# Attention scores in four 32-row groups of TensorE, eight steps a tile, with the normalisation on GpSimd

## The chip, the cores and the metric

The kernel runs on one core of a Trainium2 chip. The metric is the device time of one execution in microseconds (us); less is better. The core's engines are TensorE (PE in the profile; its weight loads are listed as PEld), VectorE (DVE), ScalarE (ACT), GpSimd (POOL), and SyncE (SP), which only issues transfers.

## What is computed

Two layers, each an attention part and a feed-forward part with a tanh gate, on x and a context of 64 batches of 64 channels by 256 positions. The change touches only the first attention:

```python
q = Wq @ norm(x) + bq;  k = Wk @ ctx + bk;  v = Wv @ ctx + bv      # per batch, 64 channels
# 8 heads of 8 channels; the first 4 channels of each q and k head are rotated by position
scores = q_h.T @ k_h / sqrt(8)                                      # 256 x 256 per head
out = softmax(scores) @ v_h.T
x = x + tanh(g) * (Wo @ out + bo)
```

After it come a routed expert layer, a gated attention pool and a second feed-forward part. They are not changed.

## The kernel before

**Tiles.** Two batches make one tile of 128 partitions; there are 32 tiles. A tile has 16 heads in 4 units of 4 (`u`, `j`). `column_order` puts the channels of q and k so that partition = 32 j + 4 d + u. Scores need more precision than one fp32r product gives, so q and k are split into a high and a low part and three products are added: q_hi k_hi, q_lo k_hi, q_hi k_lo.

**Stacks.** SP's transfers write the three products below each other: `q_st` has 32 rows for each product, which hold all four heads of a unit, and `k_st` has the same 96 rows once for each head, zero where the row is another head's. So one matmul over 96 rows gives the scores of one head (L510, into `s_ps`). VectorE takes the maximum of each row (L369). The maxima, negated and split, are turned by TensorE (L461), copied by ScalarE (L409) and written as 8 more rows of `q_st`. The second pass, transposed (L527, into `st_ps`, 104 rows), has the maximum subtracted and goes to ScalarE's exponential (L422, into `e_t`). The values are multiplied with it in L546: 32 output rows per head, four heads in the four column groups of the array. A column of ones in `v_st` gives the sums of the softmax. `o_ps` is copied (L414), turned (L488), divided (L352, L356), turned back (L494), copied (L399), projected (L441), scaled (L403) and added to x by GpSimd (L254). The projections of q and k are L433, of v L471; their rotation is L295, their split on GpSimd L260, L268, L270.

**Order.** `body(n, c, i)` on every engine is a fixed list of 16 steps `s_`; bodies run for n = -2 to 33, and are a loop unrolled four times in between. Body n computes maxima for tile n+1 (one pair of heads in every other step, L510), transposed scores for tile n (one head a step, `LAG` = 8 steps into the body), projections for tile n+2, and the output of tile n-1. All projections, turns and the output use one PSUM bank, `misc`, in turn. `s_ps` and `st_ps` have two buffers each, `e_t` eight. Every engine executes its list in order, so a wait holds up all that is behind it. SP's list of a body: the context of tile n+3, the maxima rows of tile n, then 6 of the k transfers, 3 of q and 6 of k for tile n+2. GpSimd's list: variance and rstd of tile n+2, the addition to x of tile n-2, the split of k, the split of q.

Of the kernel before, what the change touches and what calls it, by code (L numbers as in the profile page):

```python
# [67 lines left out]
def attention(nc, dram, x, ident, tanh_gain):  # L68
# [6 lines left out]

    HP = 2 * HEADS
    LAG = 8
    ROWS, MROWS = 96, 104
    PEEL_FIRST, PEEL_LAST = (-2, -1, 0, 1), (30, 31, 32, 33)

    with ExitStack() as ctx:
# [6 lines left out]
        def sem(name):  # L88
# [4 lines left out]
        bias = sb("bias", [P, 5])  # L93
        bias_v = sb("bias_v", [P, P])
        rope = sb("rope", [P, 2, D])
        own_head = sb("own_head", [P, UH])
        gains = sb("gains", [P, 4])
        out_bias = sb("out_bias", [P, 1])
        half = sb("half", [P, 1])

# [4 lines left out]
        rstd = sb("rstd", [P, 1])  # L105
        xn = sb("xn", [P, D])
        roped = {a: sb(f"{a}_roped", [P, 2, D]) for a in "qk"}
        whole = {a: sb(f"{a}_whole", [P, D]) for a in "qk"}
# [7 lines left out]
        e_t = [sb(f"e_t{r}", [P, 2, D]) for r in range(8)]  # L116
# [6 lines left out]
        s_ps = [ps(f"s_ps{r}", [P, 4, D]) for r in range(2)]  # L123
        st_ps = [ps(f"st_ps{r}", [P, 2, D]) for r in range(2)]
# [4 lines left out]
        x_first_in, x_rest_in = sem("x_first_in"), sem("x_rest_in")  # L129
        c_loaded = [sem(f"c_loaded{r}") for r in range(RING)]  # L130
        q_stacked = [sem(f"q_stacked{r}") for r in range(RING)]
        k_stacked = [[sem(f"k_stacked{j}_{r}") for r in range(RING)] for j in range(UH // 2)]
        m_stacked = [sem(f"m_stacked{r}") for r in range(RING)]
        names = ("values_cleared first_cleared others_cleared ones_set own_set tanh_ready bias_ready half_set "
                 "stats_raw stats_done eps_added rstd_ready xn_ready "
                 "q_projected q_roped q_summed q_high q_split k_projected k_roped k_summed k_high k_split "
# [27 lines left out]
        def st_head(s_):  # L164

            return (0, s_ - LAG) if s_ >= LAG else (-1, s_ + LAG)

# [3 lines left out]
        def _(sp):  # L171
# [3 lines left out]
            for dst, src in ((w_in[:], dram["w_in"]), (bias[:], dram["bias"]), (rope[:], dram["rope"]),  # L175
                             (own_head[:], dram["own_head"])):
                sp.dma_start(dst, src).then_inc(consts_in, 16)
            sp.dma_start(x[:, 0:4, :], rows[:, 0:4, :]).then_inc(x_first_in, 16)
            for dst, src in ((bias_v[:], dram["bias_v"]), (gains[:], dram["gains"]), (ident[:], dram["ident"]),
                             (w_out[:], dram["w_out"])):  # L180
                sp.dma_start(dst, src).then_inc(more_consts_in, 16)

            def body(n, c, i):
# [6 lines left out]
                if isinstance(n, int) and n == -2:  # L190
                    for t in range(4, TILES, 14):
                        sp.dma_start(x[:, t:t + 14, :], rows[:, t:t + 14, :]).then_inc(x_rest_in, 16)
                if there(n, c, 0):
                    r = c % RING
                    sp.wait_ge(s["m_taken"], n + 1)

                    sp.dma_start(q_st[r][ROWS:MROWS, :, :].bitcast(F32),
                                 m_rows[:, :].bitcast(F32)).then_inc(m_stacked[r], 16)
                if there(n, c, 2):
                    r = (c + 2) % RING  # L200

                    wait_count(sp, s["st_scored"], HP * (n - 1))
                    wait_alone(sp)

                    if isinstance(n, int) and n == -2:
                        sp.wait_ge(s["first_cleared"], 2)
                    if isinstance(n, int) and n == 0:
                        sp.wait_ge(s["others_cleared"], 2)

                    def stack_k(j, t, of):  # L210
                        sp.dma_start(k_st[r][32 * t + 8 * j:32 * t + 8 * j + 8, :, j, :].bitcast(F32),
                                     part["k"][32 * j:32 * j + 32, of, :].bitcast(F32)).then_inc(k_stacked[j // 2][r], 16)

                    sp.wait_ge(s["k_high"], n + 3)
                    for j in range(2):
                        stack_k(j, 0, 0)
                        stack_k(j, 1, 0)
                    sp.wait_ge(s["k_split"], n + 3)  # L220
                    for j in range(2):
                        stack_k(j, 2, 1)
                    sp.wait_ge(s["q_split"], n + 3)
                    for t, of in enumerate((0, 1, 0)):
                        sp.dma_start(q_st[r][32 * t:32 * t + 32, :, :].bitcast(F32),
                                     part["q"][:, of, :].bitcast(F32)).then_inc(q_stacked[r], 16)
                    for j in range(2, UH):
                        for t, of in enumerate((0, 0, 1)):
                            stack_k(j, t, of)
# [4 lines left out]
        def _(pool):  # L234
            nc.gpsimd.memset(half[:], -0.5).then_inc(s["half_set"], 1)
            nc.gpsimd.memset(y_sb[:], 0.0).then_inc(s["y_free"], 1)
            for r in (0, 1):
                nc.gpsimd.memset(k_st[r][0:ROWS, :, :, :].bitcast(F32), 0.0).then_inc(s["first_cleared"], 1)
            pool.wait_ge(s["half_set"], 1)

            def body(n, c, i):
                if there(n, c, 2):
                    pool.wait_ge(s["stats_done"], n + 3)

                    wait_count(pool, s["xn_ready"], n + 2)
# [9 lines left out]
                for a in "kq":  # L255
                    if there(n, c, 2):
# [6 lines left out]
                        if there(n, c, 1):  # L263

                            for of_ring in stacked:
                                pool.wait_ge(of_ring[before], (48 if a == "q" else 96) * uses(c, i, 1))
# [1910 lines left out]
```

## Time and profile before

| | us |
|---|---|
| median of 3 runs | 1567.44 (1565.45 to 1570.59) |
| the profiled execution, its own time | 1564.62 |
| its span, first to last instruction | 1562.6 |
| the first attention in it | 0 to 586 |
| mean granted TensorE clock | 0.958 of full speed |

Busy over the span: PE 93%, PEld 77%, DVE 61%, ACT 50%, POOL 34%. A busy share of PE counts matmuls whose ends are modelled, and overlapping ones once.

### The profile page before, as it was taken

The numbers are of one execution on the slowest core, as the hardware profiler recorded it, in microseconds if no ns is written. First come the engines' busy times: TensorE is split into PE (matmuls) and PEld (weight loads), VectorE is DVE, ScalarE is ACT, GpSimd is POOL, SyncE is SP. The second block draws the span as 40 slices with busy tenths as digits, with TensorE's granted clock in tenths as the row PEclk, the third lists the DMA queues.
The fourth block names the chain that finished last, engine by engine and source line by source line (L and its number), as shares of the span: only waits on it lengthen the run. The fifth ranks groups of instructions, "written<-read, shape, count | busy, mean of one in ns | idle before, by whom it ended". The sixth has DMA issues, their size and how long they took to land. (4 is left out here: it accounts for less than half of the span.)

```text
span 1562.6 us, 32056 instructions
## 1 busy us (share of the span) xinstructions
PE 1451.1 (93%) x10096; PEld 1209.4 (77%) x10097; DVE 953.7 (61%) x1817; ACT 775.4 (50%) x1425; POOL 535.0 (34%) x592
## 2 busy tenths in 40 slices
PE   3999999999999986999988999999978699999998
PEld 2777777777777755888877888888867478888887
DVE  7888887888788734776655433333324466666653
ACT  4466666666666663333223333333332656666652
POOL 4332332332333201744455443320005344455220
PEclk9999999999999995999999999999995799999999
DMA  5122122112212202211265332221125001111000
GB/s 176 57 57 62 53 55 62 54 53 62 55 52 62 54 3 77 105 41 55 71 196 190 121 94 91 91 67 54 50 57 175 27 28 41 42 42 41 15 14 28
DMA packets 89081, 106.54 MB, mean 68 GB/s; under 512 B 12208, under 2 KB 80432, under 8 KB 88368
## 3 DMA queue, kind: packets, MB, share of 16 engines
q1 hardware_dynamic: 79264, 73.60, 15.9%
q0 software_dynamic: 9744, 31.99, 6.4%
q8 instruction: 43, 0.70, 0.2%
q14 instruction: 30, 0.25, 0.0%
HBM read 54.29 MB, written 25.03 MB: 51 GB/s over the span
## 5 line engine op out<-in xcount | busy, mean ns | idle before, releaser
L422 ACT ACTIVATE e_t<-st_ps 128x512 f32<-128x512 f32 x512 | 277.9, 595 | 165.7 <-PE st_ps L527 165.2
L369 DVE TENSOR_REDUCE row_max<-s_ps 128x4 f32<-128x1024 f32 x256 | 311.0, 1217 | 32.5 <-PE s_ps L510 32.4
L510 PE MATMUL s_ps<-k_st,q_st 96*128 96x256 f32 x1024 | 196.7, 315 | 13.0 <-DMA q_st<-q_part 11.7
L527 PE MATMUL st_ps<-q_st,k_st 104*128 104x256 f32 x1024 | 170.2, 287 | 1.6 <-ACT e_t L422 1.5
L510 PEld LDWEIGHTS s_ps<-k_st,q_st 96*128 96x128 f32 x1024 | 147.4, 193 | 21.9 <-DMA q_st<-q_part 12.5
L527 PEld LDWEIGHTS st_ps<-q_st,k_st 104*128 104x128 f32 x1024 | 143.6, 189 | 6.6 <-ACT e_t L422 5.2
L546 PE MATMUL o_ps<-e_t,v_st 128*32 128x256 f32 x2048 | 137.0, 385 | 0.9 <-ACT e_t L422 0.9
L1599 POOL DMA_INDIRECT gathered_tail<-sorted_results,result_at x64 | 70.1, 1095 | 153.7 <-POOLq L2090 135.4
L1457 PE MATMUL y_ps_moe<-w_all_moe,xt_hi_moe 128*128 x568 | 113.3, 283 | 3.8 <-DVE xt_lo_moe L1276 3.8
L1836 DVE TENSOR_TENSOR h_all_tail<-silu_tail,u_ps_tail 128x512 f32<-128x512 f32 x64 | 43.9, 685 | 115.5 <-ACT silu_tail L1707 65.1
L1282 DVE TENSOR_TENSOR h_all_moe<-silu_moe,u_ps_moe 128x512 f32<-128x512 f32 x71 | 48.8, 687 | 107.2 <-PE u_ps_moe L1435 107.2
L1435 PE MATMUL g_ps_moe<-w_all_moe,xt_hi_moe 128*128 x284 | 107.0, 418 | 0.0
L972 ACT COPY y_sb_moe<-y_ps_moe 128x256 f32<-128x256 f32 x71 | 26.4, 372 | 161.4 <-PE y_ps_moe L1457 161.4
L1435 PE MATMUL u_ps_moe<-w_all_moe,xt_hi_moe 128*128 x284 | 99.8, 392 | 0.0
L1457 PEld LDWEIGHTS y_ps_moe<-w_all_moe,xt_hi_moe 128*128 128x128 f32 x568 | 92.8, 190 | 7.4 <-issue 4.7
L1272 DVE TENSOR_TENSOR xt_lo_moe<-t_ps_moe,xt_hi_moe 128x256 fp32r<-128x256 f32 x71 | 30.1, 424 | 93.2 <-ACT xt_hi_moe L959 93.0
L820 POOL DMA_INDIRECT sorted_rows<-xn_moe,slots_moe x64 | 64.6, 1009 | 62.7 <-DVE slots_moe L1075 45.5
L247 POOL TENSOR_SCALAR var_eps<-mean_var 128x1 f32<-128x1 f32 x32 | 7.5, 233 | 229.4 <-DVE mean_var L310 228.3
L546 PEld LDWEIGHTS o_ps<-e_t,v_st 128*32 128x32 f32 x2048 | 53.5, 109 | 40.1 <-ACT e_t L422 1.1
L1457 PE MATMUL y_ps_moe<-w_all_moe,xt_lo_moe 128*128 x284 | 80.1, 282 | 0.0
L1707 ACT ACTIVATE silu_tail<-g_ps_tail 128x512 f32<-128x512 f32 x64 | 38.0, 594 | 82.4 <-PE g_ps_tail L1995 82.3
L2007 PE MATMUL y_ps_tail<-w_hi_tail,h_hi_tail 128*128 128x256 f32 x256 | 73.5, 287 | 0.5 <-DVE h_lo_tail L1843 0.5
(310 smaller groups left out, 3592.6 us busy)
## 6 DMA issues: line engine op xcount, KB each, us to landing
k_st<-k_part SPq DMA_DIRECT2D x384, 32.0 KB
q_st<-q_part SPq DMA_DIRECT2D x96, 128.0 KB, 3.2
stage_moe<-in_experts POOLq DMA_DIRECT2D x21, 512.0 KB, 4.3
rows_in_moe<-sorted_rows SPq DMA_DIRECT2D x71, 128.0 KB, 2.0
sorted_results<-y_sb_moe SPq DMA_DIRECT2D x71, 128.0 KB
c_in<-in_ctx SPq DMA_DIRECT2D x33, 128.0 KB, 2.1
xn_moe<-in_ctx SPq DMA_DIRECT2D x8, 512.0 KB
context_tail<-in_ctx SPq DMA_DIRECT2D x8, 512.0 KB, 10.9
```

Source lines behind the costliest of these rows:

```text
L369: nc.vector.tensor_reduce(out, s_ps[s_ // 2 % 2][:].rearrange("p (j h) t -> p j h t", j=2), AX_X, ALU.max).then_inc(s["max_taken"], 1)
L422: nc.scalar.activation(e_t[h % 8][:], st_ps[h % 2][:], ACT.Exp, scale=float(DH) ** -0.5)\
L510: last = nc.tensor.matmul(s_ps[s_ // 2 % 2][:, 2 * (h - s_) + half_, :], q_st[r][0:ROWS, u, half_ * P:(half_ + 1) * P], k_st[r][0:ROWS, u, ...
L527: last = nc.tensor.matmul(st_ps[h % 2][:, half_, :], k_st[r][0:MROWS, u, j, half_ * P:(half_ + 1) * P], q_st[r][0:MROWS, u, :], start=True ...
L546: last = nc.tensor.matmul(o_ps[32 * j:32 * j + 32, u % 2, :], v_st[r][:, half_, u * UH + j, :], e_t[(u * UH + j) % 8][:, half_, :], start= ...
L820: pool.indirect_dma_start(out=xs[:, :], out_offset=bass.IndirectOffsetOnAxis(ap=slots[:, w, GT * j + t:GT * j + t + 1], axis=0), in_=xn[j ...
L1282: nc.vector.tensor_tensor(h_all[c % 2][:], silu[c % 2][:], u_ps[c % 2][:], ALU.mult)\
L1435: last = nc.tensor.matmul(bank[c % 2][:], t[b][:, kc * P:(kc + 1) * P], w_flat[:, bass.ds(where + ((w * 3 + kc) * PIECE + base), FF)], sta ...
L1457: last = nc.tensor.matmul(y_ps[:, 2 * ((c - 1) % 2), :], h[:, m * P:(m + 1) * P], w_flat[:, bass.ds(where + ((w * 3 + 2) * PIECE + m * D), ...
L1599: pool.indirect_dma_start(out=gathered[r][:], out_offset=None, in_=ys[:, :], in_offset=bass.IndirectOffsetOnAxis(ap=result_at[:, q // GT, ...
L1836: nc.vector.tensor_tensor(h_all[m % 2][:], silu[m % 2][:], u_ps[n % 2][:], ALU.mult)\
L2007: last = nc.tensor.matmul(y_ps[:, t, :], h[:, m, t * P:(t + 1) * P], w[:, m * D:(m + 1) * D], start=(m == 0 and b == 0 and t % 2 == 0), st ...
```

## The change

In words: the stacks are laid out by head. Rows 32 j to 32 j + 31 of `q_st` and `k_st` belong to head j of a unit: 8 channels by four rows, which are q_hi k_hi, q_lo k_hi, q_hi k_lo, and for two of the 8 channels a fourth row with the maxima (a zero in `q_st` until they are known, a one in `k_st`). A score is then a matmul over 32 rows, and heads j lie in different row groups of the array. A body has 8 steps. In each, TensorE issues eight score matmuls: for each half of the positions two transposed ones (heads of tile n, `LAG` = 5) and two plain ones (heads of tile n+1), whose four row groups and four PSUM banks differ. Then come 4 value matmuls (half a unit; 8 instructions, as each fp32 one is two), then one of the other jobs. `st_ps` has now one buffer, of two heads, and the exponential covers 128 x 1024. `k_st` shrinks from 4096 to 1024 columns, `k` takes 3 transfers a tile, not 12, `q` 3 and a small one of zeros.

Off VectorE: the normalised x (two GpSimd operations, one tile earlier), the bias of q and k (added on GpSimd, `turned_bias`), the two additions of the v bias (v is copied by ScalarE; its bias goes through `w_out` into `out_bias`). The two rotations of q, and of k, are one operation of 512 columns each. GpSimd's list is now: split of k, split of q, addition to x, normalisation of tile n+3.

```diff
-    LAG = 8
+    STEPS = HP // 2
+    LAG = 5
+    MAX_ROWS = slice(3, P, 16)
...
-        k_st = [sb(f"k_st{r}", [P, UNITS, UH, D], F32R) for r in range(RING)]
+        k_st = [sb(f"k_st{r}", [P, UNITS, D], F32R) for r in range(RING)]
...
-        st_ps = [ps(f"st_ps{r}", [P, 2, D]) for r in range(2)]
+        st_ps = ps("st_ps", [P, 2, 2, D])
...
@@ SP, body
+                if there(n, c, 2):
+                    wait_count(sp, s["st_scored"], STEPS * (n - 1))
+                    sp.dma_start(q_st[r][MAX_ROWS, :, :].bitcast(F32), zero_rows[:, :, :].bitcast(F32))
...
                     sp.wait_ge(s["k_high"], n + 3)
+                    for t in range(2):
+                        sp.dma_start(k_st[r][t:P:4, :, :].bitcast(F32), part["k"][:, 0, :].bitcast(F32))
...
+                    sp.wait_ge(s["q_high"], n + 3)
+                    for t in (0, 2):
+                        sp.dma_start(q_st[r][t:P:4, :, :].bitcast(F32), part["q"][:, 0, :].bitcast(F32))
...
@@ GpSimd
+            def normalize(n, k):
+                pool.wait_ge(s["stats_done"], n + k + 1)
+                nc.gpsimd.tensor_tensor(like_row(n, centered), x_row(n + k), mean_var[:, 0:1] ..., ALU.subtract)
+                nc.gpsimd.tensor_scalar(var_eps[:], mean_var[:, 1:2], EPS, None, ALU.add)
+                nc.gpsimd.tensor_tensor(rstd[:], var_eps[:], half[:], ALU.pow)
+                wait_count(pool, s["q_projected"], n + k)
+                nc.gpsimd.tensor_tensor(xn[:], centered[:], rstd[:].to_broadcast([P, D]), ALU.mult)
...
             def body(n, c, i):
+                    parts_of("k", n, c, i)
+                    parts_of("q", n, c, i)
...
+                    pool.wait_ge(s["y_taken"], n - 1)
+                    nc.gpsimd.tensor_tensor(row, row, like_row(n, y_sb), ALU.add)
...
+                    normalize(n, 3)
@@ VectorE
+                nc.vector.tensor_tensor(roped[a][:].rearrange("p a t -> p (a t)"), misc[:],
+                                        rope[:].rearrange("p a t -> p (a t)"), ALU.mult)
...
+                for p in range(STEPS):
+                    if p == 0 and there(n, c, 0): split_max(n, c)
+                    if there(n, c, 1): take_max(n, c, p)
+                    if p == 0 and there(n, c, 2): rope_parts("k", n, c)
+                    if p == 2 and there(n, c, 2): rope_parts("q", n, c)
+                    if p == 4 and there(n, c, -1): normalize_out(n, 0)
+                    if p == 5 and there(n, c, 3): stats_of(n, 3)
+                    if p == 7 and there(n, c, -1): normalize_out(n, 1)
@@ ScalarE: the exponential comes first in each step; then
+                    p == 1: m_rows; p in (2, 6): o_sb; p == 3: a_t; p == 5: y_sb; p == 6: v_st (copy 128x256)
@@ TensorE
+            def score_step(n, c, i, p):
+                if turned:
+                    wait_count(pe, s["exp_done"], STEPS * (n + k) + t)
+                    wait_alone(pe)
+                if plain:
+                    if p == 0:
+                        pe.wait_ge(q_stacked[(c + 1) % RING], 64 * uses(c, i, 1))
+                        pe.wait_ge(k_stacked[(c + 1) % RING], 48 * uses(c, i, 1))
+                    wait_count(pe, s["max_taken"], (n + 1) * STEPS + p - 1)
+                for at in range(0, 4, 2):
+                    for of, done in ((turned, "st_scored"), (plain, "scored")):
+                        for out, w, moving in of[at:at + 2]:
+                            last = nc.tensor.matmul(out, w, moving, start=True, stop=True)
...
+                for p in range(STEPS):
+                    score_step(n, c, i, p)
+                    use_values(n, c, p)
+                    p == 0: k projection; 1: turn the maxima; 2: q projection; 3: turn a_sb;
+                    p == 4: turn o_sb[0]; 5: output projection; 6: v projection; 7: turn o_sb[1]
```

The lines of the diff that name several steps `p` in one line are shortened from separate `if` blocks. The first bodies also differ: VectorE clears all `k_st` (1024 columns each) and makes the rotated biases; GpSimd clears `q_st`.

## Rows read from the trace of the kernel before

**Rows 1.** Stretches of the span, as one table

```profile
core 0: us, PE busy (x) PEld busy (x) DVE busy (x) ACT busy (x) POOL busy (x), PEclk, DMA share, GB/s
0.00:24.00 24.00, 5.35 (x12) 3.30 (x13) 14.63 (x21) 15.69 (x6) 11.89 (x16) 1.00 0.83 249
200.00:500.00 300.00, 297.58 (x2730) 234.75 (x2722) 243.18 (x409) 191.87 (x376) 92.32 (x160) 1.00 0.21 56
556.00:586.00 30.00, 24.18 (x219) 14.67 (x217) 5.41 (x15) 19.84 (x40) 2.14 (x3) 0.99 0.01 2
575.00:586.00 11.00, 6.36 (x55) 3.34 (x53) 1.10 (x4) 4.91 (x10) 0.67 (x1) 0.97 0.00 1
586.00:1562.00 976.00, 901.29 (x5200) 780.98 (x5200) 503.55 (x1070) 415.94 (x747) 360.59 (x297) 0.94 0.23 73
```

**Rows 2.** One line, 200 to 500 us: duration, first and last start

```profile
L409 ACT CAST m_rows<-misc x18: 252/254/255, 211.3 to 498.6; 64x128 fp32r<-64x128 f32 x18
```

**Rows 3.** Groups by line and shape, 200 to 500 us

```profile
L369 DVE TENSOR_REDUCE row_max<-s_ps 128x4 f32<-128x1024 f32 x143 | 174.0, 1217 | 16.3 <-PE s_ps L510 16.3
L422 ACT ACTIVATE e_t<-st_ps 128x512 f32<-128x512 f32 x286 | 155.2, 595 | 92.8 <-PE st_ps L527 92.8
L546 PE MATMUL o_ps<-e_t,v_st 128*32 128x256 f32 x1152 | 77.1, 385 | 0.0
L414 ACT COPY o_sb<-o_ps 128x512 f32<-128x512 f32 x36 | 21.1, 585 | 6.0 <-PE o_ps L546 4.3
L399 ACT COPY a_t<-misc 128x256 f32<-128x256 f32 x18 | 6.7, 372 | 10.0 <-PE misc L494 10.0
L403 ACT ACTIVATE y_sb<-misc,out_bias,tanh_gain 128x256 f32<-128x256 f32 x18 | 10.2, 569 | 0.0
L295 DVE SCALAR_TENSOR_TENSOR k_roped<-misc,bias,rope 128x256 f32<-128x256 f32 x36 | 15.8, 480 | 9.0 <-PE misc L433 9.0
```

**Rows 4.** Timeline, TensorE matmuls: start us, length us, what

```profile
301.08 1.07 PE L546 MATMUL o_ps<-e_t,v_st 128*32 128x256 f32 x16
302.50 0.72 PE L510 MATMUL s_ps<-k_st,q_st 96*128 96x256 f32 x4
303.05 0.64 PE L527 MATMUL st_ps<-q_st,k_st 104*128 104x256 f32 x4
...
309.84 1.13 PE L433 MATMUL misc<-c_in,w_in 128*128 128x256 f32 x4
310.62 0.82 PE L510 MATMUL s_ps<-k_st,q_st 96*128 96x256 f32 x4
```

**Rows 5.** Timeline, TensorE weight loads beside them

```profile
301.08 0.59 PEld L546 LDWEIGHTS o_ps<-e_t,v_st 128*32 128x32 f32 x16
302.08 0.42 PEld L488 LDWEIGHTS misc<-ident,o_sb 128*128 128x128 f32 x4 [0.41 <-issue]
```

**Rows 6.** Timelines of ScalarE, PEld and PE, end of the stage

```profile
561.98 1.09 ACT L422 ACTIVATE e_t<-st_ps 128x512 f32<-128x512 f32 x2
...
562.63 0.30 PEld L527 LDWEIGHTS st_ps<-q_st,k_st 104*128 104x128 f32 x2 [0.69 <-ACT e_t L422]
...
577.71 0.74 PE L527 MATMUL st_ps<-q_st,k_st 104*128 104x256 f32 x4
...
578.25 1.09 ACT L422 ACTIVATE e_t<-st_ps 128x512 f32<-128x512 f32 x2 [0.84 <-PE st_ps L527]
```

**Rows 7.** The groups again, GpSimd, 200 to 500 us

```profile
L260 POOL TENSOR_TENSOR k_whole<-k_roped 128x256 f32<-128x256 f32 x18 | 13.2, 732 | 23.2 <-DVE k_roped L295 23.2
L249 POOL TENSOR_TENSOR rstd<-var_eps,half 128x1 f32<-128x1 f32 x18 | 10.2, 568 | 1.5
```

**Rows 8.** DMA issues, 200 to 500 us, with median us to landing

```profile
q_st<-q_part SPq DMA_DIRECT2D x54, 128.0 KB, 3.2
```

**Rows 9.** Waits, 200 to 500 us: total us, times, longest

```profile
ACT e_t L422 <- PE st_ps L527: 92.8, 125, 1.9
```

**Rows 10.** The page, its costliest groups

```profile
L1836 DVE TENSOR_TENSOR h_all_tail<-silu_tail,u_ps_tail 128x512 f32<-128x512 f32 x64 | 43.9, 685 | 115.5 <-ACT silu_tail L1707 65.1
```

More of the change, by code:

```diff
@@ L205, in body @@
[L205 to L212, printed above, removed]
@@ L223, in body @@
-                    sp.wait_ge(s["q_split"], n + 3)
[L224 to L229, printed above, removed]
+                    sp.dma_start(k_st[r][2:P:4, :, :].bitcast(F32), part["k"][:, 1, :].bitcast(F32))\
+                        .then_inc(k_stacked[r], 16)
@@ L248, in body @@
[L248 to L249 removed]
+                    parts_of("k", n, c, i)
+                if there(n, c, 2):
+                    parts_of("q", n, c, i)
                 if there(n, c, -2):
                     pool.wait_ge(s["y_taken"], n - 1)
[L252 to L253 removed]
@@ L273, in _ @@
+                    row = x_row(n - 2)
+                    nc.gpsimd.tensor_tensor(row, row, like_row(n, y_sb), ALU.add).then_inc(s["y_free"], 1)
+                if there(n, c, 3):
+                    normalize(n, 3)
             steps(pool, body)
@@ L435, in project, with scores @@
                 last.then_inc(s[a + "_projected"], 1)
-            def body(n, c, i):
-                for s_ in range(HP):
-                    if s_ == 0 and there(n, c, -2):
-                        pe.wait_ge(s["a_taken"], n - 1)
-                        nc.tensor.matmul(misc[:, 0:D], w_out[:], a_t[:], start=True, stop=True)\
-                            .then_inc(s["y_projected"], 1)
-                    if s_ == 2 and there(n, c, 2):
-                        if isinstance(n, int) and n < 2:
+            def scores(c, p):
+                r = (c + 1) % RING
+                for half_ in range(2):
+                    for at in range(2):
+                        u, j = (2 * p + at) // UH, (2 * p + at) % UH
+                        rows = slice(32 * j, 32 * j + 32)
+                        yield (s_ps[p % 2][:, at, half_, :], q_st[r][rows, u, half_ * P:(half_ + 1) * P],
+                               k_st[r][rows, u, :])
@@ new lines, in body @@
+                    if p == 4 and there(n, c, -1):
+                        if there(n, c, -2):
+                            pe.wait_ge(s["a_taken"], n - 1)
+                        else:
+                            pe.wait_ge(s["q_roped"], n + 3)
+                        pe.wait_ge(s["o_taken"], 2 * (n - 1) + 1)
+                        turn_out(0)
+                    if p == 5 and there(n, c, -2):
+                        pe.wait_ge(s["a_taken"], n - 1)
+                        if there(n, c, -1):
+                            pe.wait_ge(s["o_normed"], 2 * (n - 1) + 1)
+                        nc.tensor.matmul(misc[:, 0:D], w_out[:], a_t[:], start=True, stop=True)\
+                            .then_inc(s["y_projected"], 1)
@@ L552, in _, with value_bias @@
-            steps(pe, body)
+                        pe.wait_ge(s["o_normed"], 2 * (n - 1) + 1)
+                        pe.wait_ge(s["o_taken"], 2 * n)
+                        turn_out(1)
+            def value_bias():
+                pe.wait_ge(more_consts_in, 3 * 16)
+                pe.wait_ge(s["v_stored"], 1)
+                nc.tensor.matmul(misc[:, 0:1], w_out[:], bias[:, 5:6], start=True, stop=True)\
+                    .then_inc(s["value_bias_made"], 1)
+            steps(pe, body, None, value_bias)
```

500 lines of the change are left out of this document (248 added, 252 removed).

## The prediction, made before the changed kernel was run

> **What bounds the kernel now.** I read the stretches first, then the groups of the steady stretch, then its timeline, then the end of the stage. The stretches [rows 1] show that the first attention ends at 586 us and that the 976 us after it have nothing to do with the change. From 200 to 500 us TensorE is busy 297.6 of 300 us, VectorE 243.2, ScalarE 191.9, GpSimd 92.3, at full clock. One tile takes (498.6 - 211.3) / 17 = 16.90 us [rows 2]. ScalarE waits 92.8 us of these 300, all for the transposed scores [rows 9]; TensorE waits for nobody. So TensorE's own list is the bound, and I have to take it apart.
>
> Busy time does not do that, since matmuls overlap; distances between starts do. Four score matmuls take 303.05 - 302.50 = 0.55 us, 0.14 each [rows 4]; 64 a tile are 8.8 us. A burst of 16 value matmuls takes 1.00 us, from its start at 301.08 to the next load at 302.08 [rows 4, 5]; four a tile are 4.0. What is left, 4.1 us, is the eight other jobs with the changes between them: a projection of k or q takes 310.62 - 309.84 = 0.78 each [rows 4], which leaves (4.1 - 1.56) / 6 = 0.42 for each of the other six.
>
> **What the rows say of tiling the array.** A value matmul lasts 385 ns [rows 3], yet 16 of them fit in 1.07 us [rows 4]: four column groups really work side by side. At the end of such a burst the loads stand still for 0.41 us before the next job can load [rows 5]. That is the price of leaving the column groups, and the change makes twice as many such bursts. Row groups do not occur in this trace. Their gain has to be bounded: from none (0.14 us a matmul) to the four at a time of the column groups. I take four at a time, since the nearest row is the same array used in 32-wide groups, and the change sends each round to four different banks. [...]
>
> **The change, part by part: TensorE.** Eight scores go out in two rounds of four. After a wait, two score matmuls one after the other lead to the start of the exponential in 578.25 - 577.71 = 0.54 us [rows 6]; two rounds should take the same, and some hundredths for the stagger, 0.56. The next job's loads can begin about 0.1 before, at 0.45. A value burst is now half as long and there are eight. Its price lies between half of 1.00 = 0.50 and half of the loads plus the whole stand, 0.30 + 0.41 = 0.71 [rows 5]; I take 0.60. The other job costs 0.78 at steps 0 and 2 and 0.42 at the rest. Going back to row groups costs something between 0 and 0.41; I take 0.25. Sums: 0.45 + 0.60 + 0.25 + 0.78 = 2.08 us at steps 0 and 2, 1.72 at the other six: 14.5 us a tile.
>
> **ScalarE's loop.** `st_ps` has one buffer now. So exponential, next scores, next exponential form a chain. The exponential of 1024 columns: a copy of 256 takes 372 ns, of 512 585 [rows 3], so 213 for 256 more; 595 + 2 x 213 = 1.02 us. After an exponential TensorE loads 0.05 later: the first of the two that begin at 561.98 ends at 562.575, the load starts at 562.63 [rows 6]. So 1.02 + 0.05 + 0.56 = 1.63 us a step at least, 13.0 a tile. This lies below TensorE's 1.72, so TensorE's list decides, but only just. ScalarE's other work has 0.05 + 0.56 = 0.61 us in each step, while the scores are made. `o_sb` (0.585) fits, `y_sb` (0.569) nearly; at step 6 `o_sb` and the new copy of v come to 0.585 + 0.37 = 0.96 (v as the copy of 256 columns to `a_t`, [rows 3]), so the next exponential starts 1.02 + 0.56 + 0.96 = 2.54 us after the scores began, which means a step of 1.98, 0.26 more than 1.72. Together 14.5 + 0.26 = 14.8 us a tile. The extra wait on VectorE's maximum that now stands ahead of the transposed matmuls too is held at nothing, as `s_ps` has two buffers and VectorE is a step behind at most.
>
> **VectorE.** It loses the normalised x and the v additions. What stays: eight maxima at 1.217 = 9.7 us [rows 3], two rotations of 512 PSUM columns at 0.685 [rows 10], where four of 0.48 stood [rows 3]. The rest (statistics, split, division) I take from the difference: 243.2 us in 300 are 13.7 a tile; 13.7 - 9.7 - 4 x 0.48 = 2.1, from which the removed ones come off. So VectorE needs 11.1 to 13.2 us. That is cover, not bound, if TensorE comes at 14.8; it is the next in line.
>
> **GpSimd.** Nine operations on 256 columns at 0.73, two copies at no more, rstd 0.57 [rows 7]: 8 to 9.2 us a tile. It has the time. Its order matters: k and q are split ahead of the addition, which waits for step 5. q is rotated about 2.8 us after the start of step 2; add, add, copy, subtract at up to 0.73 end 2.9 later; the stack lands 3.2 after [rows 8]. That is 8.9 us, plus an issue or two, about 10 after step 2 starts; the next body starts 14.8 - 2.08 - 1.72 = 11.0 after it. One us of slack. Had the addition come first, it would have held q to the end of step 5, 3 or 4 us later. The transfers carry what they carried, in 9 issues and not 17, so SP's queue gets shorter.
>
> **Start and end.** To 24 us only twelve matmuls run [rows 1]; large clears of `k_st` and twelve small k transfers stand ahead. They shrink, the new clears and bias operations add some back. I take 6 us off, between 0 and 12. At the end (556 to 586, [rows 1]) the chain of one buffer replaces two; I take no change.
>
> **The sum.** (16.90 - 14.8) x 30 full tiles = 63; with 6 at the start, 69 us. The profiled execution took 1564.62 (span 1562.6 and 2.0 around it) and would be 1496. The median is 2.8 above it, 1567.4 - 69 = 1498.
>
> **Rival 1: the switches cost more.** The trace's 0.41 of standing loads [rows 5] speaks for it. [...] Price: 0.27 us at each of the two changes that I held at nothing or at 0.25, so a step is 0.45 + 0.27 + 0.60 + 0.27 + other job, 12.7 + 4.1 = 16.8 us a tile with all, or 16.1 where the other jobs' 4.1 already holds their part. At 16.1: 1567 - 24 - 6 = 1537. At 0.41 each it would pass 16.9 and end slower. [...]
>
> **Rival 2, slower: row groups load one after the other.** What decides is whether a load of 128 weight columns can run beside another row group's. Value loads have only 32 columns, so the rows do not prove it. If they cannot, eight scores go at 0.14: the sixth ends 0.54 + 4 x 0.14 = 1.10 after the start, and ScalarE's loop is 1.02 + 0.05 + 1.10 = 2.17. TensorE: 0.45 + 6 x 0.14 = 1.29, with 0.60 + 0.25 makes 2.14 + other job, 17.1 + 4.1 = 21.2 us a tile at worst, 19.5 if the changes cost nothing. At 19.5: 1567 + 78 - 6 = 1639. It turns slower as soon as the scores take (16.9 - 14.8) / 8 = 0.26 us a step longer than two rounds.
>
> **Rival 3: better.** If a half value burst costs 0.50 and the return to row groups nothing, ScalarE's chain decides: 13.0 plus 0.35 at step 6 and 0.5 at steps 0 and 2; 13.6 a tile gives 1567 - 99 - 6 = 1462. The q chain of 10 us after step 2 would then have no slack left, so it cannot be much less.
>
> **Rival 4: q comes late, or nothing changes.** If GpSimd runs slower beside VectorE, body starts wait for `q_stacked` and the tile stays near 16.9: 1561.
>
> **The clock.** TensorE will have gaps of tenths of a us in each step. It had such at the end of the stage, 58% busy, at a granted clock of 0.97 [rows 1]. [...]
>
> **How the numbers follow.** Forecast 0.60 (tile 14.2 to 15.5), rival 1 0.16, rival 2 0.11, rival 3 0.10, rival 4 0.03. Range: from rival 3's 1462 to 1550, which takes in most of rival 1. Left out: rival 2, rival 4, the ends. A measurement here can tell 0.3% (4.7 us) from no change. Faster: 0.60 + 0.10 + 0.15 = 0.85; same: 0.03; slower: 0.12.
>
> **What would show it.** Right: score matmuls starting in fours a few ns apart, 16 value loads become 8, the restart of scores 0.05 after an exponential, copies of `m_rows` 14.8 us apart, exponential near 1.02 us, VectorE's maxima never waited for long. Wrong: score matmuls 0.1 or more apart (rival 2), idle loads of 0.3 us at most changes (rival 1), TensorE waiting for q's transfers at body starts (rival 4), or a clock under 0.9 in the stage.

## The result, and the profile after

The changed kernel took 1518.99 us (median of 4 runs, 1517.46 to 1523.47) beside 1567.76 for the kernel before: ratio 0.969, 95% interval 0.967 to 0.972. It is 48.8 us faster where 69 were forecast. The profiled execution took 1523.47, with a span of 1521.6.

The stretches of the changed kernel answer to [rows 1]; its first attention ends at 539 us, not 586 (columns as there).

```profile
24.00:54.00 30.00, 24.34 (x129) 14.89 (x127) 24.41 (x29) 5.10 (x7) 14.26 (x24) 0.62 0.20 66
200.00:500.00 300.00, 271.89 (x3068) 140.66 (x3068) 251.69 (x358) 208.85 (x282) 149.99 (x249) 1.00 0.20 63
...
500.00:506.00 6.00, 4.33 (x51) 2.16 (x47) 2.85 (x6) 4.30 (x6) 0.46 (x1) 0.98 0.01 3
506.00:533.00 27.00, 26.01 (x159) 11.31 (x160) 1.65 (x6) 14.34 (x17) 0.73 (x1) 0.50 0.01 2
533.00:540.00 7.00, 2.99 (x18) 1.32 (x18) 0.55 (x2) 2.09 (x4) 1.45 (x2) 0.99 0.00 0
```

TensorE now has gaps (271.9 of 300 us, before 297.6) and the other engines are busier. The granted clock is lower in two stretches. While the stage starts it is 0.62 on average, where the kernel before had 0.89 in the same window:

```profile
24.00:54.00 30.00, 22.49 (x121) 17.87 (x121) 24.93 (x37) 4.14 (x9) 9.01 (x16) 0.89 0.23 61
```

From 506 to 533 us, where only the last exponentials and their values are left, it is 0.50. The clock records of every trace here hold 1.00 or 0.50 and nothing else, so a mean such as 0.62 is a mixture of the two.

The copies of `m_rows` answer to [rows 2]:

```profile
L423 ACT CAST m_rows<-misc x17: 246/246/247, 207.5 to 449.0; 64x128 fp32r<-64x128 f32 x17
```

A tile takes (449.0 - 207.5) / 16 = 15.09 us, before 16.90. The last of these 16 are no longer bodies of the loop: bodies 26 to 33 are written out behind it, and they are shorter. From copy to copy the loop alone takes (389.4 - 207.5) / 12 = 15.16, the written-out bodies (477.9 - 434.5) / 3 = 14.47. This difference is used below. The groups by line and shape, 200 to 500 us (answering to [rows 3]):

```profile
L361 DVE TENSOR_REDUCE row_max<-s_ps 128x4 f32<-128x1024 f32 x162 | 197.8, 1221 | 31.2 <-PE s_ps L498 30.1
L417 ACT ACTIVATE e_t<-st_ps 128x1024 f32<-128x1024 f32 x161 | 165.0, 1025 | 88.7 <-PE st_ps L498 86.6
L514 PE MATMUL o_ps<-e_t,v_st 128*32 128x256 f32 x1288 | 102.9, 391 | 0.0
L498 PE MATMUL st_ps<-q_st,k_st 32*128 32x256 f32 x644 | 80.6, 325 | 28.1 <-ACT e_t L417 17.5 <-DVE row_max L361 7.4
L342 DVE TENSOR_TENSOR q_roped<-misc,rope 128x512 f32<-128x512 f32 x19 | 13.1, 691 | 7.0 <-PE misc L456 7.0
L266 POOL TENSOR_TENSOR xn<-centered,rstd 128x256 f32<-128x256 f32 x19 | 11.7, 616 | 1.5
```

One step in the timeline (answering to [rows 4, 5]; start, length, what, and the idle time ahead of it with its releaser):

```profile
300.67 0.18 PEld L498 LDWEIGHTS st_ps<-q_st,k_st 32*128 32x128 f32 x2 [0.33 <-DVE row_max L361]
300.67 0.38 PE L498 MATMUL st_ps<-q_st,k_st 32*128 32x256 f32 x2
300.67 0.18 PEld L498 LDWEIGHTS s_ps<-k_st,q_st 32*128 32x128 f32 x2
300.67 0.39 PE L498 MATMUL s_ps<-k_st,q_st 32*128 32x256 f32 x2
300.77 0.19 PEld L498 LDWEIGHTS st_ps<-q_st,k_st 32*128 32x128 f32 x2
...
300.89 0.28 PE L498 MATMUL st_ps<-q_st,k_st 32*128 32x256 f32 x2
300.90 0.28 PE L498 MATMUL s_ps<-k_st,q_st 32*128 32x256 f32 x2
...
301.11 0.64 PE L514 MATMUL o_ps<-e_t,v_st 128*32 128x256 f32 x8
301.21 1.02 ACT L417 ACTIVATE e_t<-st_ps 128x1024 f32<-128x1024 f32 x1 [0.58 <-PE st_ps L498]
...
301.68 0.20 PEld L561 LDWEIGHTS misc<-ident,a_sb 128*128 128x128 f32 x2 [0.41 <-DVE q_roped L342]
...
302.46 0.19 PEld L498 LDWEIGHTS st_ps<-q_st,k_st 32*128 32x128 f32 x2 [0.59 <-issue]
```

Four score matmuls start together, the next four 0.22 us later, and the burst of values after 0.44 us. The exponential begins at 301.21 and ends at 302.24, but the next scores load at 302.46, about 0.23 later. That gap matters below.

**Where the time went** (spans, before to after). The first copy of `m_rows` comes at 39.8 and not at 43.1 us: -3.3. From the first to the last copy 465.8 and not 519.8 us: -54.0 (forecast -63). From the last copy to the end of the stage 33.7 and not 23.1: +10.6. All that follows: 982.2 and not 976.6: +5.6. Together -41.0. The medians lie 48.8 apart, since the profiled execution of before was among the fastest of its kernel and that of after was the slowest of its four.

### The profile page after: what moved, and what is told of

Its sections match the earlier page's. It is cut to its first block and busy times, and to the rows that moved or that the text cites. A ratio compares the mean times of both kernels' runs of the same rounds, so it can differ in the third digit from the quotient of the medians.

```text
span 1521.6 us, 31047 instructions
## 1 busy us (share of the span) xinstructions
PE 1372.3 (90%) x10098; PEld 1025.4 (67%) x10099; DVE 919.2 (60%) x1665; ACT 751.9 (49%) x1197; POOL 616.3 (41%) x722
## 5 line engine op out<-in xcount | busy, mean ns | idle before, releaser
L417 ACT ACTIVATE e_t<-st_ps 128x1024 f32<-128x1024 f32 x256 | 262.3, 1025 | 154.1 <-PE st_ps L498 151.0
L498 PE MATMUL st_ps<-q_st,k_st 32*128 32x256 f32 x1024 | 132.9, 336 | 48.9 <-ACT e_t L417 30.9
L514 PE MATMUL o_ps<-e_t,v_st 128*32 128x256 f32 x2048 | 169.8, 404 | 0.0
L498 PEld LDWEIGHTS st_ps<-q_st,k_st 32*128 32x128 f32 x1024 | 81.1, 190 | 121.5 <-issue 72.5
L498 PE MATMUL s_ps<-k_st,q_st 32*128 32x256 f32 x1024 | 131.4, 338 | 8.5 <-DMA q_st<-q_part 6.5
L1333 DVE TENSOR_TENSOR h_all_moe<-silu_moe,u_ps_moe 128x512 f32<-128x512 f32 x71 | 48.8, 687 | 108.6 <-PE u_ps_moe L1486 108.3
L498 PEld LDWEIGHTS s_ps<-k_st,q_st 32*128 32x128 f32 x1024 | 78.0, 190 | 12.3 <-DMA q_st<-q_part 6.8
L995 ACT ACTIVATE silu_moe<-g_ps_moe 128x512 f32<-128x512 f32 x32 | 19.1, 598 | 107.1 <-PE g_ps_moe L1404 107.1
L1018 ACT ACTIVATE silu_moe<-g_ps_moe 128x512 f32<-128x512 f32 x71 | 42.5, 599 | 59.6 <-PE g_ps_moe L1486 59.5
```

Of the source, the lines that this page charges most:

```text
L417: nc.scalar.activation(e_t[t % 4][:], st_ps[:], ACT.Exp, scale=float(DH) ** -0.5)\
L498: last = nc.tensor.matmul(out, w, moving, start=True, stop=True)
L514: last = nc.tensor.matmul(o_ps[32 * j:32 * j + 32, u % 2, :], v_st[r][:, half_, u * UH + j, :], e_t[(2 * u + j // 2) % 4][:, j % 2, half_, :],
L1333: nc.vector.tensor_tensor(h_all[c % 2][:], silu[c % 2][:], u_ps[c % 2][:], ALU.mult)\
```

## The experiments

The edits are made to the changed kernel. The medians stand with the ratio to the kernel before; the tile is the distance between copies of `m_rows` from 200 to 450 us. An edit that adds or takes away lines shifts the line numbers.

**Same row group back to back.**

```diff
-                for at in range(0, 4, 2):
-                    for of, done in ((turned, "st_scored"), (plain, "scored")):
-                        for out, w, moving in of[at:at + 2]:
+                for of, done in ((turned, "st_scored"), (plain, "scored")):
+                    if of:
+                        for out, w, moving in (of[0], of[2], of[1], of[3]):
```

> The eight score matmuls of a step are issued with the two of one row group behind each other, so five slots are needed instead of two. Theory A (the gain comes from four row groups at once): each step's scores take 0.33 us longer on TensorE and the transposed ones end 0.11 later; the steps' copies of the maxima go from 15.15 us apart to about 17.7, the time from 1519 to about 1600. Rival (row groups add little, the gain is that of eight longer steps and less VectorE work): no more than 0.3 us a tile, under 1530.

1527.3 us, 0.974 [0.971, 0.978]; a tile of 15.2. The number is the rival's (under 1530), but it does not speak against the row groups, since the edit did not take the concurrency away. The timeline tells why:

```profile
299.88 0.39 PE L498 MATMUL st_ps<-q_st,k_st 32*128 32x256 f32 x2 [0.50 <-ACT e_t L417]
299.90 0.39 PE L498 MATMUL s_ps<-k_st,q_st 32*128 32x256 f32 x2
300.10 0.28 PE L498 MATMUL st_ps<-q_st,k_st 32*128 32x256 f32 x2
300.12 0.28 PE L498 MATMUL s_ps<-k_st,q_st 32*128 32x256 f32 x2
```

The program issues all four transposed matmuls ahead of the plain ones. In the trace the plain ones of the free row groups start 0.02 us after the first two, ahead of the transposed ones issued before them. Matmuls of different row groups overtook each other here, so the order of issue inside a step was no handle on the concurrency. The row groups themselves have to be changed. (The median is 8 us above the changed kernel's; between the first and last copy of `m_rows` the traces differ by 1.9 us, and the rest was not traced.)

**Two row groups, and one.** These two compute scores of the wrong heads: heads 2 and 3 get those of heads 0 and 1, and with one group all four get head 0's. The work is the same.

```diff
-rows = slice(32 * j, 32 * j + 32)
+rows = slice(32 * (j % 2), 32 * (j % 2) + 32)
```

With one group it is `j % 1`.

> Heads 0 and 2 use row group 0, heads 1 and 3 row group 1 (scores of the wrong heads for half of them): four rounds of two. Theory A: a step's scores 0.24 us longer on TensorE, 0.12 to 0.24 later for the exponential; a tile about 16.7 us, the time about 1569, as before the change. Rival: 15.1 us, 1519.

> All score matmuls read rows 0 to 31, so all eight of a step are in one row group and heads 1 to 3 of a unit get head 0's scores; everything else is as in the change. Theory A (four at a time is the gain): eight turns of 0.12 us, TensorE's step 0.71 us longer, the exponential starts 1.0 us after the first load instead of 0.54; a tile about 20.5 us, the time about 1686, slower than before. Rival (the row groups are not what counts): 15.1 us, 1519.

Two groups: 1557.31 us (ten runs, 1553 to 1578), 0.995 [0.992, 0.999], tile 16.3. One group: 2037.37, 1.297 [1.293, 1.300], tile (416.9 - 225.0) / 6 = 32.0. Timeline of two groups, then of one, then the stretch from 200 us of one:

```profile
300.71 0.38 PE L498 MATMUL st_ps<-q_st,k_st 32*128 32x256 f32 x2
300.93 0.28 PE L498 MATMUL s_ps<-k_st,q_st 32*128 32x256 f32 x2
301.05 0.28 PE L498 MATMUL st_ps<-q_st,k_st 32*128 32x256 f32 x2
301.16 0.29 PE L498 MATMUL s_ps<-k_st,q_st 32*128 32x256 f32 x2
301.38 0.64 PE L514 MATMUL o_ps<-e_t,v_st 128*32 128x256 f32 x8
```

```profile
300.03 0.79 PE L498 MATMUL st_ps<-q_st,k_st 32*128 32x256 f32 x2
300.62 0.62 PE L498 MATMUL s_ps<-k_st,q_st 32*128 32x256 f32 x2
301.05 0.62 PE L498 MATMUL st_ps<-q_st,k_st 32*128 32x256 f32 x2
301.47 0.62 PE L498 MATMUL s_ps<-k_st,q_st 32*128 32x256 f32 x2
302.03 1.08 PE L514 MATMUL o_ps<-e_t,v_st 128*32 128x256 f32 x8
```

```profile
200.00:500.00 300.00, 299.39 (x1423) 191.64 (x1423) 121.39 (x168) 101.33 (x130) 70.99 (x119) 0.53 0.10 31
```

With two groups a step needs four rounds of two, and first load to value burst is 0.67 us and not 0.44. The tile is 1.25 us longer for it, and of the 1.81 us gained a tile 0.56 are left. So most of the gain of the change is the step from two row groups to four, as forecast. With one group the matmuls go one by one, 0.21 apart, but this is not the price of the missing groups alone: the granted clock is 0.53, so most of the stretch ran at the lower level, 0.50 (the value burst shows it too, 1.08 us for 0.64). The expectation had the full clock and missed by 350 us. Early in the same trace, from 62.7 to 66.1 us, the granted clock was 1.00 (a value burst takes 0.64 us there), and one step shows the price of the groups by itself:

```profile
64.70 0.47 PE L498 MATMUL st_ps<-q_st,k_st 32*128 32x256 f32 x2 [0.17 <-ACT e_t L417]
...
65.81 0.82 PE L514 MATMUL o_ps<-e_t,v_st 128*32 128x256 f32 x8
```

Eight scores take 1.11 us and not 0.44, that is 2.5 times as long; the 0.67 more are near the 0.71 that the expectation had for it. So in this step, at full clock, the price of the groups was as expected. The tile of 32.0 us was taken at a clock of 0.53; how its excess over the expected 20.5 divides between the clock and the rest was not measured.

**The order of the waits.** The changed kernel waits for the exponential, then for VectorE's maximum. In the loop the counts of both waits are computed from the loop's index, in the written-out bodies they are constants. Between the two waits stands a `nop`. The author's estimate was that the restart of the scores, 0.23 us after the exponential, pays for a count computed behind the first wait; no view of the profile lists such work, so only the times can speak for it. Turned round:

```diff
                 if turned:
-                    wait_count(pe, s["exp_done"], STEPS * (n + k) + t)
-                    wait_alone(pe)
                 if plain:
...
                     wait_count(pe, s["max_taken"], (n + 1) * STEPS + p - 1)
+                    wait_alone(pe)
+                if turned:
+                    wait_count(pe, s["exp_done"], STEPS * (n + k) + t)
```

> TensorE waits for VectorE's maximum first, alone, and for the exponential in front of the first score matmul itself. Theory A (ScalarE's chain of 1.025 + 0.225 + 0.54 us a step decides, and 0.17 of the 0.225 is TensorE's sequencer working out the second count after the wait): restart after an exponential falls to 0.05 to 0.11 us, a tile in the loop from 15.15 to 14.3 +- 0.2, the time by about 20 us to 1499. Theory B (VectorE, busy 252 of 300 us, decides): no change, within 3 us of 1519.

The 0.17 us in it is an estimate: about the 0.225 of the changed kernel's trace less the 0.05 of [rows 6]. What the traces show in its place follows below, 0.12 and 0.06.

1486.75 us, 0.948 [0.945, 0.951]: 32 us better than the changed kernel, and more than expected. The tile is (436.1 - 210.8) / 16 = 14.08. Its timeline:

```profile
301.46 1.02 ACT L417 ACTIVATE e_t<-st_ps 128x1024 f32<-128x1024 f32 x1 [0.67 <-PE st_ps L498]
...
302.54 0.18 PEld L498 LDWEIGHTS st_ps<-q_st,k_st 32*128 32x128 f32 x2 [0.39 <-ACT e_t L417]
```

The exponential ends at 302.48 and the scores load 0.06 later. The medians lie 32 us apart, the two profiled spans 38.7: of these 28.6 lie between the first and the last copy of `m_rows`, 5.3 between the last and the end of the stage, where the low clock lasted for 7 us and not 27, and 4.7 behind the stage. Step by step, worked out from the single instructions of the traces (median over 16 tiles, us: length of the step, and from the end of the exponential to its first load):

```
step                     0     1     2     3     4     5     6     7    sum
changed, length       2.07  1.80  2.07  1.80  1.76  1.88  1.80  1.91  15.08
changed, after exp    0.34  0.50  0.23  0.50  0.23  0.19  0.23  0.23
turned round, length  2.07  1.62  2.07  1.62  1.68  1.72  1.65  1.65  14.08
turned round, after   0.05  0.50  0.05  0.50  0.05  0.11  0.05  0.08
```

The steps 0 and 2, which hold a projection and where TensorE's list decides, are the same. The six others were bound by ScalarE's loop, which had become 1.02 + 0.54 + 0.23 = 1.79 us; they fall to 1.62 to 1.72. The length of step 7 contains the gap of 0.34 ahead of step 0, where the waits for the stacks also stand behind the first one.

The edit moved the `nop` as well as the count, so by itself it does not tell which of them cost the time. The written-out bodies of the changed kernel do: they have the same waits in the same order with the same `nop`, but every count is a constant.

```profile
471.42 1.02 ACT L417 ACTIVATE e_t<-st_ps 128x1024 f32<-128x1024 f32 x1
...
472.56 0.21 PEld L498 LDWEIGHTS st_ps<-q_st,k_st 32*128 32x128 f32 x2
```

There the scores load 0.11 us after the exponential (the most frequent gap of the three tiles from 436 to 478 us), in the loop 0.23, with the waits turned round 0.05. So 0.12 of the 0.18 us is the difference between bodies of the loop and bodies with constant counts (0.23 and 0.11), and 0.06 that between the two orders (0.11 and 0.05), with the `nop` and the second wait behind the exponential or ahead of it. Ahead of step 0 it is 0.34 in the loop and 0.22 behind it, again 0.12.

**The waits apart.** The transposed matmuls wait for the exponential only and go first; then the wait on the maximum and the plain ones.

```diff
                 if turned:
                     wait_count(pe, s["exp_done"], STEPS * (n + k) + t)
+                    for out, w, moving in turned:
+                        last = nc.tensor.matmul(out, w, moving, start=True, stop=True)
                 if plain:
                     wait_count(pe, s["max_taken"], (n + 1) * STEPS + p - 1)
+                    for out, w, moving in plain:
+                        last = nc.tensor.matmul(out, w, moving, start=True, stop=True)
```

> In each step the four transposed score matmuls go first and wait for the exponential alone; then the four plain ones wait for VectorE's maximum. No wait stands ahead of another any more. If the order of the two waits is all that e2 changed (the count worked out after the exponential), e12 comes out as e2: tile 14.08 us, 1487. If VectorE's maxima also held up the transposed scores in e2, e12 is below it, 13.8 or less, 1478. If the plain matmuls now come too late to share the rounds, above it: 14.4 or more, 1497.

1493.98 us, 0.954 [0.952, 0.956], tile 14.4, 7 us worse than turning them round and the third of the three cases of the expectation. The second wait with its count now stands between the two groups, and the plain matmuls start 0.09 us after the transposed ones (301.51 after 301.42 in one step) and not 0.01, the value burst begins 0.52 and not 0.44 us after the first load, and the steps 0 and 2, bound by TensorE, take 2.26 and 2.16.

**Fewer switches.** With the waits turned round, values in bursts of 16 in every other step.

```diff
+                    if t % 2 == 0:
+                        return
                     pe.wait_ge(s["exp_done"], STEPS * (n + k) + 2 * u + 2)
-                    for j in range(UH):
+                    for half_ in range(2):
+                        for j in range(UH):
...
```

> The wait order of e2, and the value matmuls of a whole unit in one burst of 16 every other step, so four entries into the column groups and four stands fewer a tile. If the changes of the array's shape are what TensorE (busy 241 of 250 us in e2) loses: two half bursts of 0.57 become one of 1.00, 0.57 us a tile less on its list, the tile from 14.08 to about 13.6, the time about 1473. Rival (ScalarE's chain and VectorE decide; a burst of 1.00 in one step makes that step late): 14.1 us or more, 1487 or more.

1537.06 us, 0.978 [0.975, 0.982], tile 15.7: worse than eight bursts by 1.6 us a tile. The steps with a burst take 2.50 (0 and 2), 2.02 and 2.08, the ones without fall to ScalarE's 1.62 and no lower, with one of 1.70. So four switches fewer gained nothing here. The long bursts fell in the even steps, on top of the two projections; in the odd steps they were not tried. An estimate from the same rows for that, 4 x 2.05 + 4 x 1.62 = 14.7 us, still lies above the 14.08 of eight bursts.

**The end of the stage.** For n = 31 and 32, where no maxima are left to take, four idle score matmuls are added to each step; nobody reads them.

```diff
+                if isinstance(n, int) and n in (31, 32):
+                    if (n, p) == (31, 0):
+                        pe.wait_ge(s["max_taken"], TILES * STEPS)
+                        wait_alone(pe)
+                    for out, w, moving in scores(c, p):
+                        nc.tensor.matmul(out, w, moving, start=True, stop=True)
```

> In bodies 31 and 32, where no plain scores are left, each step issues four score matmuls more into the idle s_ps, whose result nobody reads. Theory C (the stage's last 33.7 us, from the last copy of the maxima to its end, are 10 us longer than before because the granted clock fell to 0.5 there when the plain scores stopped): clock 1.0 down to the last steps, the end 24 us, the time 1509. Rival (the single st_ps buffer makes the end long): clock may stay but the end keeps 30 us or more, the time 1517 to 1521.

1513.5 us, 0.965 [0.962, 0.968]; from the last copy of `m_rows` to the end 27.0 us and not 33.7. Its stretch:

```profile
506.00:533.00 27.00, 19.97 (x232) 9.90 (x232) 2.20 (x8) 16.29 (x23) 2.07 (x3) 1.00 0.01 2
```

More matmuls (232 for 159), less busy time, full clock: work that nobody needs makes the kernel faster. So at least 6.7 of the 10.6 us went with the low clock. Why 27.0 and not 23.1 is open; one buffer for `st_ps` is a candidate, and it wasn't tried.

**Both.** Waits turned round and the busy end.

> The wait order of e2 and the extra matmuls of e4 together. If the two gains are of different places they add: tile 14.08 us, the end of the stage from 28.4 to about 24, the time about 1482 (e2: 1486.75; e4 took 5.5 off). Rival: e2's end had most of its clock already, so nothing is added, 1487.

1484.18 us, 0.945 [0.943, 0.947], the lowest median, though the 2.6 us to the turned waits alone lie inside the spread of the runs. The busy end is worth little here (26.4 us for 28.4), since with the waits turned round the clock fell for 7 us only, 492.8 to 499.6.

**VectorE as cover.** One more `bn_stats` of 0.42 us a tile, its result unused, on the changed kernel and on the one with the waits turned round.

```diff
+                nc.vector.bn_stats(spare[:], x_row(n + k)).then_inc(s["spare_made"], 1)
```

> The change with one more statistics operation a tile on VectorE (0.42 us and its wait), result unused. Theory A (VectorE is cover, idle 2.4 us of a 15.15 us tile): under 0.1 us a tile, under 1522. Theory B (VectorE decides): 0.42 us a tile or more, 1532 or more.

> The same extra VectorE operation in e2, where VectorE is busy 223.9 of 250 us, idle 1.5 us of a 14.08 us tile. Theory A: under 0.15 us a tile, under 1491.5. Theory B: once the wait order is mended VectorE decides, 0.42 us a tile, about 1500.

1515.56 us, 0.967 [0.965, 0.970], tile 15.09; and 1492.2, 0.951 [0.948, 0.953], tile 14.08. Neither tile moved, so VectorE, busy for 251.7 of 300 us in the changed kernel, is cover in both. Whether the change had needed to take the normalisation and the v additions off VectorE was not tested; this shows only that 0.42 us more would fit. The second is 5 us above its base, and its end shows where:

```profile
478.00:505.00 27.00, 26.43 (x160) 11.14 (x156) 1.65 (x6) 14.36 (x18) 0.73 (x1) 0.50 0.01 2
```

The end ran at the low clock again, 34.0 us for 28.4. Small shifts decide whether it does.

**GpSimd's order.** The addition to x ahead of the split of q, as it stood in the kernel before (there it was ahead of the split of k too). The normalisation stays on GpSimd.

```diff
-                if there(n, c, 2):
-                    parts_of("q", n, c, i)
                 if there(n, c, -2):
...
                     nc.gpsimd.tensor_tensor(row, row, like_row(n, y_sb), ALU.add).then_inc(s["y_free"], 1)
+                if there(n, c, 2):
+                    parts_of("q", n, c, i)
```

> GpSimd adds to x ahead of the split of q, as the old order had it. Theory A (the q chain then starts at step 5's end: y_sb ends 11.9 us after a body's start, add 0.73, four operations 3.1, transfers about 3.2): TensorE waits at each body start for q's transfers, a tile takes about 18.9 us, the time about 1635. Rival (transfers are hidden anyway): 15.15 us, 1519.

1668.56 us, 1.063 [1.059, 1.067], tile (439.0 - 213.4) / 11 = 20.5. Waits, 200 to 500 us: total, times, longest:

```profile
PE st_ps L498 <- DMA q_st<-q_part: 52.2, 15, 3.6
```

Once a tile TensorE waits 3.5 us for q's transfer; the prediction had q held up by 3 or 4. And TensorE is busy for 236.0 us of 300 at a mean clock of 0.83, which the expectation (1635) did not have: the low clock is part of the 20.5. The order is worth 150 us, what the clock cost included: without it the change would lose.

## Why the prediction was right, and by how much it was off

**Direction and mechanism: right.** The row groups do work four at a time, in the changed kernel's timeline, and two experiments that took them away lost most or all of the gain. A score went from 0.14 us [rows 4] to 0.44 / 8 = 0.055, 2.5 times the rate; with one row group at full clock it was 1.11 / 8 = 0.14 again. Rival 2 (loads one after the other) is out: the first four loads all start at 300.67 in the timeline above, the next four 0.10 later. Whether the four different banks of a round have a part in it was not tested.

**TensorE's terms: right to 0.03 us.** Scores 0.44 (0.45 forecast), half a value burst 0.57 (0.60), a k projection with the return to row groups 311.98 - 310.92 = 1.06 (0.78 + 0.25 = 1.03), step 0 2.07 (2.08). Exponential 1.025 (1.02), first load to exponential 0.54 (0.56).

**The restart after the exponential: wrong, the costliest term in the loop.** It was taken as 0.05, from [rows 6]: the kernel before, at the end of its stage, where the transposed matmuls wait for the exponential and no second wait comes behind it. In the changed kernel's loop it was 0.23, and 0.34 ahead of step 0. The same error stands a second time in the prediction, where the extra wait on VectorE's maximum was "held at nothing": not because a maximum came late, but because a second wait stands behind the exponential's, with a count computed in the loop. What was measured: turning the waits round took 1.0 us off the tile, all of it in the six light steps and none in the two that TensorE bounds, and the written-out bodies, with constant counts, restart after 0.11 with the order unchanged and take 14.47 us a tile for 15.16. The profile names VectorE's `row_max` as the releaser of these loads, or "issue"; a wait for several semaphores is put down to the last event. The step table speaks against the maximum: with its wait ahead of the exponential's the restart fell from 0.23 to 0.05.

**Step 6 and the light steps: too dear.** With the gap gone the six light steps take 9.94 us together; forecast 6 x 1.72 + 0.26 = 10.58. The 0.26 at step 6 did not appear: in ScalarE's timeline of the changed kernel

```profile
306.64 1.02 ACT L417 ACTIVATE e_t<-st_ps 128x1024 f32<-128x1024 f32 x1
...
307.57 0.58 ACT L428 COPY o_sb<-o_ps 128x512 f32<-128x512 f32 x1
...
308.03 0.39 ACT L444 COPY v_st<-misc 128x256 f32<-128x256 f32 x1
...
308.44 1.03 ACT L417 ACTIVATE e_t<-st_ps 128x1024 f32<-128x1024 f32 x1
```

`o_sb` begins 0.09 us before the exponential ends and `v_st` 0.12 before `o_sb` ends, so both fit while the scores of 307.90 are made. The sum added whole lengths. The forecast of 1.72 for TensorE's list was also some hundredths above the 1.62 to 1.72 measured. The two errors partly cancelled, and that the tile came so near, 15.09 against 14.8, is in part luck: 54.0 us from the first to the last copy, where the sum had 63.

**The end: held at nothing, was +10.6 us.** The prediction allowed for no fall of the clock, from a stretch with TensorE 58% busy at 0.97. In the changed kernel it was granted 0.50 over 27 us in that part of the stage; with idle matmuls added it was 1.00 and the end 6.7 us shorter. At the start, where -3.3 came of the -6, the clock was low too, until 55.2 us by the clock's records, before until 42.6. What that cost was not separated. The traces whose clock records reach back that far have it too, until 55 to 67 us, and in the others the column's 1.00 is no evidence against it. The run with one more statistics operation on the changed kernel, its stretch and two projections of k and q:

```profile
24.00:54.00 30.00, 25.00 (x127) 15.31 (x125) 25.01 (x31) 5.10 (x7) 14.26 (x24) 1.00 0.20 66
...
36.25 2.08 PE L460 MATMUL misc<-c_in,w_in 128*128 128x256 f32 x4
...
56.93 1.13 PE L460 MATMUL misc<-xn,w_in 128*128 128x256 f32 x4
```

Four matmuls of one shape take 2.08 and later 1.13 us. The changed kernel's trace, whose clock records reach back that far, shows both lengths beside both levels, 2.08 inside the stretch at 0.50 (to 55.2 us) and 1.13 behind it:

```profile
31.30:55.20 23.90, 19.96 (x113) 12.12 (x117) 19.10 (x24) 5.10 (x7) 10.71 (x19) 0.50 0.24 76
55.20:62.00 6.80, 5.79 (x69) 2.94 (x73) 5.51 (x6) 4.72 (x6) 4.92 (x8) 1.00 0.19 63
...
52.38 2.08 PE L456 MATMUL misc<-c_in,w_in 128*128 128x256 f32 x4
57.40 1.13 PE L456 MATMUL misc<-xn,w_in 128*128 128x256 f32 x4
```

So the projection at 36.25 us in the other run is read as one at 0.50. That trace's first clock record stands at 54.1 us, and ahead of it the column prints 1.00. "A clock under 0.9 in the stage" was named as what would show the prediction wrong, and so it was, for those two stretches. The remaining +5.6 us lies behind the stage, in code that the change does not touch; the runs of this case show 975.5 to 983.5 us for it, 976.6 before. The mean granted clock there was 0.93, before 0.94; it was not traced further.

**Rivals.** Rival 1 (more expensive switches) is not borne out as a rival: the idle loads are there, 0.41 leaving the column groups and 0.33 returning, but the return was priced at 0.25 and cost 0.28, and halving the bursts' number did not pay where it was tried. Its 0.27 us for each change was the author's estimate and no run shows it; the runs showed the two idle times and the return at 0.28. Rival 3 (better, 1462) is where the experiments went: 1484 with both edits, and its tile of 13.6 against 14.08. Two of the prediction's sums do not come out as written: rival 3's terms, 13.0 + 0.35 + 0.5, are 13.85 and would give 1470, and rival 2's tile without the price of the changes is 21.2 - 8 x 0.25 = 19.2 and not 19.5. The forecast does not rest on either; the lower end of the range does on the first. Rival 4 is real as a mechanism: moving the addition ahead of q produced it, at 1669 and not at the 1561 it was given. A GpSimd that runs slower beside VectorE was not seen: its first operation of the split of k took 732 ns before and 726 after, with VectorE busy for 243.2 and 251.7 of 300 us.

**VectorE, GpSimd.** VectorE 251.7 us in 300, 12.7 a tile (forecast 11.1 to 13.2), not the bound. GpSimd 150.0, 7.5 a tile (forecast 8 to 9.2, though its own terms end at 8.6): the two operations of the normalisation take 616 ns and not 0.73 us, and the two copies 398 ns. No wait of TensorE for q's transfers shows from 200 to 500 us.

## What to carry to other kernels

Put the wait that comes last by time last in the program too, and directly on the instruction that needs it: here that took the restart after the exponential from 0.23 to 0.05 us and the tile from 15.08 to 14.08. With the order unchanged, bodies with constant counts restarted sooner than bodies of the loop (0.11 and 0.23 us). A term measured at the end of a stage need not hold in its middle (the restart, 0.05 and 0.23 us), so take it from the stretch where it will be used. When a change thins an engine's work, read the granted clock of the short stretches at the ends, since this stage, granted 1.00 in its middle, lost an eighth of its gain to the low clock there (6.7 of 54.0 us). Ahead of a trace's first clock record take the length of a matmul that is known at both levels (2.08 and 1.13 us here), not the clock's column.

## What the hardware showed that was not expected

Matmuls of different row groups start out of the order of issue: plain ones 0.02 us after the first transposed pair, though the second transposed pair stood ahead of them in the program.

The clock fell where the profile has TensorE busiest, and not only where it has gaps. With one row group it was busy for 299.4 of 300 us at a granted clock of 0.53. At the end of the stage, after 6 us with TensorE busy for 4.3 at a clock of 0.98, it fell to 0.50 and stayed there for 27 us, 26.0 of them busy; with 73 matmuls more in the same stretch it was granted 1.00 and was busy for 20.0. With two row groups, 284 of 300 us busy, it had 1.00. With the addition ahead of q, where TensorE waits once a tile, it was busy for 236.0 of 300 at 0.83. A busy share is itself made longer by the low clock (a value burst takes 1.08 us for 0.64), so it is not the row to judge the clock by. Why the clock is low with one row group was not tested.

With the same two waits and `nop` behind the exponential, the scores load 0.23 us after it in the loop, where the counts are computed, and 0.11 in the written-out bodies, where they are constants: 0.12 between them. With only the exponential's wait behind it, it is 0.05, 0.06 less. Ahead of step 0, with the waits for the stacks there too, it is 0.34 in the loop and 0.22 behind it.
